# The opening of the attention stage: order of its loads, its first norm, its late tiles and the place of batch 1's norm

## The chip, the core and the metric

One core of a Trainium2 chip runs the whole kernel in one launch. TensorE (PE) multiplies matrices into PSUM, eight banks of 512 float32 columns on 128 partitions. VectorE (DVE) and ScalarE (ACT) read PSUM; GpSimd (POOL) works on SBUF and requests gathers; SyncE (SP) issues most transfers. Each engine runs its own instructions in the order in which they were written and waits on semaphores. The metric is the device time of the launch in microseconds; the median of three runs of the kernel before is 1331.42.

## The reference

Four batches of 512 tokens with 512 features go through four gated blocks. The third is cross attention, and the change lies where the second, a mixture of experts with a shared expert, passes over to it.

```
x = x + tanh(g_ffn[0]) * ffn0(layernorm(x))         # 8 routed experts, top 2, and a shared one
x = x + tanh(g_xattn[1]) * xattn(layernorm(x), ctx)  # 32 heads of 16
x = x + tanh(g_ffn[1]) * ffn1(layernorm(x))          # 8 experts, top 2

xattn: q = rope(x @ Wq, pos);  k, v = split(ctx @ Wkv);  k = rope(k)
       w = softmax(q k^T / 4) per head;  out = (w v) @ Wout + bout
```

## The kernel before

X (16 tiles of 128 tokens, four per batch) stays in SBUF. The stage before leaves three things to `attention`: the routed rows in DRAM (`f_y`), which each tile still has to gather (two rows per token) and add; the shared expert of the last eight tiles ("late tiles", numbered 0 to 7 in `LateTiles`, tiles 8 to 15 of X), whose turned input lies in DRAM (`f_xT`, two halves of 1 MB); and K and V.

`Combine` gathers and adds the routed rows. Its `pool` (L1576) makes POOL request two gathers of 256 KB per tile into one of `ring` pairs of buffers; a request waits until the tile that last used the pair is added. Its `vector` (L1590) adds them on VectorE, L1594 and L1596.

A late tile goes through `up` (PE, four products, L1961), `silu` (ACT, L1969), `gate` (VectorE, L1975), `turn` (PE, L1980), `take` (ACT, L1987), `down` (PE, two products, L1995) and `add` (VectorE, L2003). In the table `LATE` they stand as u, g, t, d and y, per turn and slot. The inputs of the late tiles are loaded into `a_attnT` and `a_wo`.

Attention works in 16 units (b, c): batch b, eight heads c. Its program is a chain of turns (b, c) from (-1, 0) to (4, 0), each with 8 steps or 16 slots. In turn (b, c) PE makes the scores of unit (b, c) (L2830), ACT their exponentials (L2986), PE the values (L2864); beside them PE makes the maximum products of the next units (L2849), two products per slot, which VectorE reduces (L3191). Maximum products of unit (0,0) begin in slot 8 of turn (-1,2), scores in turn (0,0). `jobs` puts side jobs into slots: q is the projection (L2765, q of unit (0,0) in turn (-1,1)), x the transposes of the normalized rows (L2759), m the transposes of the cut maxima (L2771), o and a those of the output, p the output projection (L2789). All but p of the last batch go through PSUM bank 7, so that each waits for the one before it to be copied out.

q of a unit is scaled by ACT (`a_qf`, L2958), its pairs are swapped (VectorE, L3093), it is rotated with the table `a_tab` and cut into three bf16 parts (`rotate_and_cut`, L1908 to L1921; VectorE for the first unit, POOL for all others), stored by SP and loaded again as `a_Q`. For the first unit ACT issues half of these loads, after which it has to load the table of Silu (L1969).

On VectorE a turn's tasks hang in slots. A turn with a norm has statistics of a tile in slots 0 to 3 (L3053), the aggregate in 4 (L3060), reciprocal and normalization in 8 (L3065, L3071), and in 12 `add_bias`: scale `a_tbias` once (L3078), which waits for its load, and add it to the batch (L3081). ACT's Sqrt is in step 3 (L3001). `batch_to_norm` gives batch 0 to turn (-1,0), batch 1 to (-1,3), batch 2 to (0,3), batch 3 to (1,3). `tiles_to_add` gives two routed tiles, in slots 10 and 14, to (-1,0), (-1,1) and to (0,0) up to (0,3).

SP's opening loads are f_xT's first half, Wq (1 MB), the rotation table (512 KB), twelve pieces of K and one of V for unit 0 (64 KB each and 512 KB), the same for unit 1, tbias and f_xT's second half.

## Time and profile before

| | us |
|---|---|
| median of 3 runs | 1331.42 |
| lowest, highest | 1329.64, 1335.47 |
| the profiled execution | 1335.91 |
| its span | 1334.1 |
| PE busy in the span | 1174.2 |
| DVE, ACT, POOL busy | 830.4, 666.2, 397.7 |

Times in the rows are microseconds from the start of the span, of one profiled execution. The stage of attention begins at 569.53 in it. A float32 product of 128x512 shows as two MATMUL records. PEclk is the granted clock of TensorE as a share of 2.4 GHz: 0.50 is the 1.2 GHz level. The chain of waits is followed back from the last instruction. A busy engine doesn't tell by itself what bounds a stretch; the rows are read for what ended each wait.

### The profile page before, as it was taken

The page shows a single profiled execution, that of the slowest core. Times are in us where ns is not written, and L with a number is a line of the kernel's source. Part 1 is how long each engine was busy: PE and PEld are TensorE (multiplying, and loading weights), DVE is VectorE, ACT ScalarE, POOL GpSimd, SP SyncE. Part 2 cuts the span into 40 slices and gives each one's busy share as a digit, 9 for nine tenths or more (in the row PEclk, how much of TensorE's full clock was granted, in tenths as well). Part 3 has the DMA queues.
Part 4 walks back from the last instruction along what each step waited for, and adds up shares of the span by engine and source line. Part 5 has one row for each costly group of instructions (what it writes and reads, how often), then busy time and mean ns, then how long its engine had stood idle before and what let it go on. Part 6 is the DMA issues. An engine that isn't in the chain of part 4 may idle for free.

```text
span 1334.1 us, 16599 instructions
## 1 busy us (share of the span) xinstructions
PE 1174.2 (88%) x5308; PEld 511.9 (38%) x5309; DVE 830.4 (62%) x1283; ACT 666.2 (50%) x1175; POOL 397.7 (30%) x469
## 2 busy tenths in 40 slices
PE   5776876897999999958799989999999999889998
PEld 3454443564444444423232223222322222234543
DVE  6787865244455554135988888778777777624543
ACT  2575564564222222235456666566656556662453
POOL 4455631001222222033234432222223233101332
PEclk8988997999899999977999999999999999998999
DMA  7324125654444444194324342222222225300011
GB/s 247 129 91 134 56 95 195 223 192 159 150 147 154 147 147 135 56 277 112 113 85 132 116 124 72 85 81 81 68 85 80 81 81 66 46 0 9 33 40 48
DMA packets 111029, 145.79 MB, mean 109 GB/s; under 512 B 24952, under 2 KB 79736, under 8 KB 110440
## 3 DMA queue, kind: packets, MB, share of 16 engines
q1 hardware_dynamic: 91816, 113.47, 26.6%
q0 software_dynamic: 18368, 28.85, 8.4%
q10 hardware_dynamic: 768, 2.49, 0.5%
q8 instruction: 42, 0.69, 0.2%
q14 instruction: 35, 0.29, 0.1%
HBM read 99.54 MB, written 48.37 MB: 111 GB/s over the span
## 4 chain that ended last, share of the span: by engine, by line
PE 33%; DVE 8%; issue 8%; ACT 7%; POOL 1%; DMA 0%; ACTq 0%; POOLq 0%; DVEq 0%
PE PS L2864 8%; PE PS L2830 6%; PE PS L2765 5%; PE PS L2849 4%; PE PS L2789 3%; DVE a_top L3191 3%; ACT shared_w L2986 3%; PE PS L2368 2%; ACT a_E L2986 2%; PE PS L2391 1%; PE PS L1961 1%; POOL a_K L2128 1%; DVE a_early L3071 1%; PE PS L2759 1%; DVE X L3139 0%
## 5 line engine op out<-in xcount | busy, mean ns | idle before, releaser
L3191 DVE TENSOR_REDUCE a_top<-PS 128x2 f32<-128x1024 f32 x256 | 308.8, 1223 | 89.5 <-PE PS L2849 83.2
L2830 PE MATMUL PS<-a_Q,a_K 99*128 99x512 bf16 (+1 forms) x512 | 167.5, 387 | 18.7 <-ACT a_E L2986 4.2
L2986 ACT ACTIVATE shared_w<-PS 128x512 f32<-128x512 f32 x256 | 138.8, 596 | 80.1 <-PE PS L2830 77.2
L2986 ACT ACTIVATE a_E<-PS 128x512 f32<-128x512 f32 x256 | 138.9, 596 | 63.0 <-PE PS L2830 59.7
L1481 PE MATMUL PS<-f_W,f_GT 128*128 x312 | 141.8, 598 | 0.0
L2849 PE MATMUL PS<-a_K,a_Q 64*128 64x512 bf16 x512 | 100.4, 389 | 7.8 <-DVE a_top L3191 7.2
L2830 PEld LDWEIGHTS PS<-a_Q,a_K 99*128 99x128 bf16 (+1 forms) x512 | 44.5, 98 | 155.2 <-issue 50.8
L1908 POOL TENSOR_TENSOR a_qf<-a_qf,a_tab 128x512 f32<-128x512 f32 x15 | 19.1, 1272 | 282.3 <-DVE a_swapped L3093 282.3
L1537 DVE TENSOR_TENSOR f_H<-f_SG,PS 128x256 f32<-128x256 f32 x39 | 16.4, 421 | 125.5 <-ACT f_SG L1521 125.5
L1481 PEld LDWEIGHTS PS<-f_W,f_GT 128*128 128x128 f32 x312 | 57.0, 193 | 57.3 <-issue 57.3
L2765 PE MATMUL PS<-a_xT,a_early 128*128 128x512 f32 x128 | 72.3, 661 | 2.1 <-ACT a_xT L2952 0.7
L1500 PE MATMUL PS<-f_W,f_HT 128*128 x156 | 73.2, 593 | 0.0
L2789 PE MATMUL PS<-a_wo,a_attnT 128*128 128x512 f32 x128 | 70.5, 657 | 1.4 <-ACT a_attnT L2974 0.8
L1521 ACT ACTIVATE f_SG<-PS 128x256 f32<-128x256 f32 x39 | 15.0, 384 | 110.2 <-PE PS L1481 110.2
L2864 PE MATMUL PS<-shared_w,a_V 128*32 128x512 f32 x512 | 69.7, 617 | 0.0
L2864 PE MATMUL PS<-a_E,a_V 128*32 128x512 f32 x512 | 68.7, 609 | 0.0
L2849 PEld LDWEIGHTS PS<-a_K,a_Q 64*128 64x128 bf16 x512 | 24.6, 93 | 111.2 <-issue 69.7
L2128 POOL TENSOR_TENSOR a_K<-a_Q,a_tab 128x512 bf16<-128x512 f32 x32 | 33.3, 1041 | 108.7 <-DVE a_Q L2228 108.7
L2368 PE MATMUL PS<-a_early,a_Q 128*128 128x512 bf16 x256 | 60.5, 379 | 0.0
L1527 ACT COPY f_Y<-PS 128x512 f32<-128x512 f32 x39 | 22.9, 587 | 60.4 <-PE PS L1500 60.4
L2228 DVE TENSOR_TENSOR a_Q<-a_Q,PS 128x512 f32<-128x512 f32 x32 | 22.0, 686 | 47.2 <-ACT a_Q L2289 47.2
L1447 POOL DMA_INDIRECT f_G<-f_xn,f_idx x39 | 41.9, 1073 | 29.5 <-POOL f_idx L1444 28.7
(379 smaller groups left out, 2058.1 us busy)
## 6 DMA issues: line engine op xcount, KB each, us to landing
f0r_raw<-in_L_ffn_W_dram SPq DMA_DIRECT2D x24, 512.0 KB, 4.5
a_K<-k_parts SPq DMA_DIRECT2D x192, 64.0 KB, 2.3
a_Q<-a_q_parts SPq DMA_DIRECT2D x186, 64.0 KB
f_y<-f_Y SPq DMA_DIRECT2D x39, 256.0 KB
v_units<-V SPq DMA_DIRECT2D x16, 512.0 KB, 2.9
a_V<-v_units SPq DMA_DIRECT2D x16, 512.0 KB, 3.6
k_parts<-f_k_parts SPq DMA_DIRECT2D x16, 384.0 KB, 3.4
a_q_parts<-a_parts SPq DMA_DIRECT2D x16, 384.0 KB, 2.8
```

What stands on the lines that cost most here:

```text
L1447: pool.indirect_dma_start(out=G[k][:], out_offset=None, in_=xn_dram, in_offset=bass.IndirectOffsetOnAxis(ap=idx[:, k:k + 1].bitcast(U32), ...
L1481: last = nc.tensor.matmul(PS[:, 2 + k % 2, 0:2 * I], GT[k][:, c, :], W13[:, bass.ds(e, 1), c, :].rearrange("p a n -> p (a n)"), start=(c = ...
L1500: last = nc.tensor.matmul(PS[:, 6 + k % 2, :], HT[k][:, c, :], W2[:, bass.ds(e, 1), c, :].rearrange("p a n -> p (a n)"), start=(c == 0), s ...
L2128: self.nc.gpsimd.tensor_tensor(self.H[j % 2][:, h * HE:(h + 1) * HE, :], self.HF[h], gate, ALU.mult).then_inc(self.h_ready, 1)
L2368: last = nc.tensor.matmul(PS[:, 2 * h + m, :], self.xb[b % 2][:, c, t * P:(t + 1) * P], self.W13[:, c, m, h * HE:(h + 1) * HE, :].rearrang ...
L2765: last = nc.tensor.matmul(B, wq[:, extra, c * P:(c + 1) * P], xT[:, extra, :], start=(extra == 0), stop=(extra == DC - 1))
L2789: last = nc.tensor.matmul(bank_of(kind, unit, extra), attnT[b % 2][:, d, t * P:(t + 1) * P], wo[:, d, :], start=(d == 0), stop=(d == DC - 1))
L2830: nc.tensor.matmul(PS[:, 4 + h % 2, :], K6[k][0:rows_, o, head // 2, kt * P:(kt + 1) * P], Q6[k][0:rows_, o, head // 2, :], start=True, st ...
L2849: last = nc.tensor.matmul(PS[:, 2 * pair + o, :], Q6[k][at, o, h // 2, t * P:(t + 1) * P], K6[k][at, o, h // 2, :], start=True, stop=True)
L2864: last = nc.tensor.matmul(PS[32 * h:32 * h + 32, 6, :], V[k][:, kt, (step // 4) * 4 + h, :], E[step % 2][:, h, :], start=(kt == 0), stop=( ...
L2986: nc.scalar.activation(E[step % 2][:, h, :], PS[:, 4 + h % 2, :], ACT.Exp).then_inc(exp_done, 1)
L3191: nc.vector.tensor_reduce(top[:, h - h % 2:h - h % 2 + 2, t], PS[:, 2 * pair:2 * pair + 2, :], AX.X, ALU.max).then_inc(maxed, 1)
```

## The change

- `Combine` in attention gets four pairs of buffers instead of three.
- SP waits for the first tile's add before it issues Wq, and for the third tile's before the rotation table and all that follows. The second half of f_xT moves ahead of unit 1's K and V; tbias stays behind them and is now last.
- Each half of f_xT is loaded in four pieces with a semaphore each, and `up` waits per piece.
- VectorE takes the statistics of batch 0 behind each tile's adds, and aggregates and normalizes before its first turn. Gate 0 stands behind tile 1, gate 1 behind tile 2.
- The x transposes of batch 0 alternate between banks 7 and 3. Late tile 2's down product goes to bank 6 instead of 2; the first maximum products wait for three late adds.
- In `LATE` only half of tile 2's `up` is done before the turns; it and the other tiles stand later.
- Batch 1's norm moves from turn (-1,3) to (0,0), its x transposes to slots 10, 12, 13, 14. The routed adds of (0,0) to (0,3) move to (0,1) to (1,0).

```diff
-    DOWN = (6, 0, 1, 2, 6, 6, 6, 6)
+    DOWN = (6, 0, 1, 6, 6, 6, 6, 6)
...
     def load(self, sp, k):
-        sp.dma_start(self.homes[k], self.xT_dram[k]).then_inc(self.loaded[k], 16)
+        for c in range(self.DC):
+            sp.dma_start(self.homes[k][:, c, :], self.xT_dram[k][:, c, :]).then_inc(self.loaded[k][c], 16)
...
-        if c == 0:
-            if t == 0:
-                pe.wait_ge(self.loaded[k], 16)
-            if n >= 2:
-                pe.wait_ge(self.HT_ready, n - 1)
+        if t == 0:
+            pe.wait_ge(self.loaded[k][c], 16)
+        if c == 0 and n >= 2:
+            pe.wait_ge(self.HT_ready, n - 1)
...
-        rows = Combine(nc, sb, sem, X, F32, weights, pos, ffn_gate, ys, 3, [attnT[1][:, d, :] for d in range(DC)])
+        rows = Combine(nc, sb, sem, X, F32, weights, pos, ffn_gate, ys, 4, [attnT[1][:, d, :] for d in range(DC)])
...
-                for d, when in enumerate((6, 7, 8, 10)):
+                for d, when in enumerate((10, 12, 13, 14) if b == 0 else (6, 7, 8, 10)):
...
-        LATE = {(-1, 0): {9: [("g", 2, 0), ("y", 0, 0), ("y", 1, 0), ("t", 2, 0)]},
...
+        LATE = {(-1, 0): {9: [("y", 0, 0), ("y", 1, 0)]},
+                (-1, 2): {4: ups(2, [2, 3]) + ups(3), 5: [("g", 2, 0), ("t", 2, 0)] + downs(2), 7: [("y", 2, 0), ("g", 3, 0)],
...
+            if kind == "x" and unit[0] == 0:
+                return PS[:, (7, 3)[extra % 2], :]
...
-            nb = {0: b + 1 if b == -1 else None, DC - 1: b + 2}.get(c)
+            nb = {0: b + 1 if b < 1 else None, DC - 1: b + 2 if b >= 0 else None}.get(c)
...
-            if b == -1 and c < 2 or b == 0:
-                first = TB + 2 * c if b == -1 else 2 * TB + 2 * c
+            turn_ = DC * b + c
+            if -DC <= turn_ < 2 - DC or 0 < turn_ <= DC:
+                first = TB + 2 * c if b == -1 else 2 * TB + 2 * (turn_ - 1)
...
             late.load(sp, 0)
+            sp.wait_ge(rows.tile_added, 1)
             sp.dma_start(wq, Wq.rearrange("(c p) n -> p c n", p=P)).then_inc(wq_loaded, 16)
...
+                    else:
+                        sp.wait_ge(rows.tile_added, TB - 1)
                     sp.dma_start(tab[0][:], tables_dram[bass.ds(unit[0], 1)].rearrange("a p k s -> p (a k) s")).then_inc(tab_loaded, 16)
...
                     load_kv(unit)
+                    late.load(sp, 1)
                     load_kv((0, 1))
...
                     sp.dma_start(tbias[:], bout.partition_broadcast(P)).then_inc(tbias_loaded, 16)
-                    late.load(sp, 1)
...
+                    if b == 0 and extra >= 2:
+                        pe.wait_ge(xT_ready, extra - 1)
...
-                        pe.wait_ge(late.added, 3 + pair)
+                        pe.wait_ge(late.added, 3)
...
+            def first_tile(t):
+                rows.vector(v, t)
+                v.wait_ge(rows.tile_added, t + 1)
+                first_norm.step(nc.vector.bn_stats(stats[:, t, :], X[:, t, :]))
...
-            rows.vector(v, 0)
+            first_tile(0)
+            first_tile(1)
             late.gate(v, 0)
-            rows.vector(v, 1)
+            first_tile(2)
             late.gate(v, 1)
-            rows.vector(v, 2)
-            rows.vector(v, 3)
+            first_tile(3)
+            first_norm.wait()
+            for t in range(TB):
+                last = nc.vector.bn_aggr(mv[:, t, :], stats[:, t, :])
...
-                        at(t, stat)
+                        if nb:
+                            at(t, stat)
...
-                    at(4, aggregate)
-                    at(8, normalize)
+                    if nb:
+                        at(4, aggregate)
+                        at(8, normalize)
                     at(12, add_bias)
```

The order of the instructions, first SP at the opening of attention (`a_attnT` and `a_wo` are the homes of f_xT's halves, `a_early` of Wq), before:

```order
L1949 DMA a_attnT<-f_xT 128x2048
L2643 DMA a_early<-in_L_xattn_Wq_dram 128x4x512
L2667 DMA a_tab<-rope_tables 128x1024
L2655 DMA a_K_0<-k_parts 16x4x512 x12
L2656 DMA a_V<-v_units 128x1024
L2655 DMA a_K_1<-k_parts 16x4x512 x12
L2656 DMA a_V<-v_units 128x1024
L2676 DMA a_tbias<-in_L_xattn_bout_dram 128x512
L1949 DMA a_wo<-f_xT 128x2048
L2683 DMA a_q_parts<-a_parts 128x3x512
```

and now:

```order
L1950 DMA a_attnT<-f_xT 128x512 x4
L2650 DMA a_early<-in_L_xattn_Wq_dram 128x4x512
L2676 DMA a_tab<-rope_tables 128x1024
L2662 DMA a_K_0<-k_parts 16x4x512 x12
L2663 DMA a_V<-v_units 128x1024
L1950 DMA a_wo<-f_xT 128x512 x4
L2662 DMA a_K_1<-k_parts 16x4x512 x12
L2663 DMA a_V<-v_units 128x1024
L2686 DMA a_tbias<-in_L_xattn_bout_dram 128x512
L2692 DMA a_q_parts<-a_parts 128x3x512
```

The second half of f_xT moved ahead of K_1; tbias is the last load ahead of the store of q's parts.

VectorE from the normalization of batch 0 (`a_early` is written) to the first rotation, before:

```order
L3071 TENSOR_SCALAR a_early<-X,a_mv,a_rstd 128x512 x4
L1975 TENSOR_TENSOR a_E<-a_E,PS 128x256
L2003 SCALAR_TENSOR_TENSOR X<-PS,tg,X 128x512 x2
L1594 SCALAR_TENSOR_TENSOR X<-a_attnT,a_tw,X 128x512
L1596 SCALAR_TENSOR_TENSOR X<-a_attnT,a_tw,X 128x512
L3078 TENSOR_SCALAR a_tbias<-a_tbias,tg 128x512
L3081 TENSOR_TENSOR X<-X,a_tbias 128x2048
L1594 SCALAR_TENSOR_TENSOR X<-a_rows,a_tw,X 128x512
L1596 SCALAR_TENSOR_TENSOR X<-a_rows,a_tw,X 128x512
L3093 STREAM_SHUFFLE a_swapped<-a_qf 128x512
L1908 TENSOR_TENSOR a_qf<-a_qf,a_tab 128x512
```

and now:

```order
L3053 TENSOR_SCALAR a_early<-X,a_mv,a_rstd 128x512 x4
L2003 SCALAR_TENSOR_TENSOR X<-PS,tg,X 128x512 x2
L1594 SCALAR_TENSOR_TENSOR X<-a_attnT,a_tw,X 128x512
L1596 SCALAR_TENSOR_TENSOR X<-a_attnT,a_tw,X 128x512
L3106 TENSOR_SCALAR a_tbias<-a_tbias,tg 128x512
L3109 TENSOR_TENSOR X<-X,a_tbias 128x2048
L1594 SCALAR_TENSOR_TENSOR X<-a_attnT,a_tw,X 128x512
L1596 SCALAR_TENSOR_TENSOR X<-a_attnT,a_tw,X 128x512
L3122 STREAM_SHUFFLE a_swapped<-a_qf 128x512
L1908 TENSOR_TENSOR a_qf<-a_qf,a_tab 128x512
L1909 TENSOR_TENSOR a_swapped<-a_swapped,a_tab 128x512
```

The bias (tbias, then X<-X,a_tbias) and one more tile's adds stand ahead of the shuffle in both.

TensorE around the first maximum products (`a_K_0,a_Q_0`), before:

```order
L1961 MATMUL PS<-shared_w,a_attnT 128x512 x4
L1961 MATMUL PS<-shared_w,a_wo 128x512 x4
L1980 MATMUL PS<-identf,a_E 128x128 x2
L1995 MATMUL PS<-shared_w,a_E 128x512 x2
L1980 MATMUL PS<-identf,a_E 128x128 x2
L2849 MATMUL PS<-a_K_0,a_Q_0 128x512 x2
L1995 MATMUL PS<-shared_w,a_E 128x512
L2849 MATMUL PS<-a_K_0,a_Q_0 128x512 x2
L1995 MATMUL PS<-shared_w,a_E 128x512
L2849 MATMUL PS<-a_K_0,a_Q_0 128x512 x2
L1961 MATMUL PS<-shared_w,a_wo 128x512
```

and now:

```order
L2770 MATMUL PS<-identf,a_early 128x128 x16
L2776 MATMUL PS<-a_xT,a_early 128x512 x8
L1961 MATMUL PS<-shared_w,a_attnT 128x512 x6
L1980 MATMUL PS<-identf,a_E 128x128 x2
L1995 MATMUL PS<-shared_w,a_E 128x512 x2
L2860 MATMUL PS<-a_K_0,a_Q_0 128x512 x2
L1980 MATMUL PS<-identf,a_E 128x128 x2
L1961 MATMUL PS<-shared_w,a_wo 128x512
L2860 MATMUL PS<-a_K_0,a_Q_0 128x512 x2
L1995 MATMUL PS<-shared_w,a_E 128x512 x2
L2860 MATMUL PS<-a_K_0,a_Q_0 128x512 x2
L1961 MATMUL PS<-shared_w,a_wo 128x512
```

Late tile 3's and 4's up products (`shared_w,a_wo` is 4's) left the place ahead of the maximum products; tile 2's turn and down products came there.

## Rows read from the trace of the kernel before

**Rows 1.** The page's part 4: the chain that ended last, shares of the span by engine.

```profile
PE 33%; DVE 8%; issue 8%; ACT 7%; POOL 1%; DMA 0%; ACTq 0%; POOLq 0%; DVEq 0%
```

**Rows 2.** A stretch: busy of PE, PEld, DVE, ACT, POOL; PE clock, DMA share, GB/s.

```profile
600.00:610.00 10.00, 6.67 (x20) 4.13 (x21) 8.20 (x12) 4.48 (x6) 2.97 (x2) 0.50 0.54 197
```

**Rows 3.** Order of time: start, length (us), engine, line, form, count, idle before.

```profile
580.67 0.75 DVE L1594 SCALAR_TENSOR_TENSOR X<-a_attnT,a_tw,X 128x512 f32<-128x512 f32 x1 [10.87 <-DMA a_attnT<-f_y,l_pos]
...
594.05 0.75 DVE L1594 SCALAR_TENSOR_TENSOR X<-a_attnT,a_tw,X 128x512 f32<-128x512 f32 x1 [4.85 <-DMA a_attnT<-f_y,l_pos]
...
601.00 1.11 PE L2759 MATMUL PS<-identf,a_early 128*128 128x128 f32 x4 [7.88 <-DVE a_early L3071]
```

**Rows 4.** Order of time, the first rotation on VectorE, its first and last step.

```profile
615.59 0.01 DVE L3093 LOAD_MASK_SELECT a_swapped<-a_qf  x1 [7.25 <-ACT a_qf L2958]
...
620.22 0.69 DVE L1921 TENSOR_TENSOR a_parts<-a_qf,a_parts 128x512 bf16<-128x512 f32 x1
```

**Rows 5.** Groups by line, VectorE, 631.5 to 676.8: count, busy us, mean ns, idle.

```profile
L3191 DVE TENSOR_REDUCE a_top<-PS 128x2 f32<-128x1024 f32 x24 | 28.9, 1217 | 3.2 <-issue 1.9 <-PE PS L2849 1.3
L3053 DVE BATCH_NORM_STATS2 a_stats<-X 128x6 f32<-128x512 f32 x4 | 2.7, 684 | 0.0
L3071 DVE TENSOR_SCALAR a_early<-X,a_mv,a_rstd 128x512 f32<-128x512 f32 x4 | 2.3, 629 | 0.0
```

**Rows 6.** Order of time, TensorE, from the first maximum products to the first score.

```profile
631.55 0.39 PE L2849 MATMUL PS<-a_K,a_Q 64*128 64x512 bf16 x2
...
634.84 1.13 PE L1961 MATMUL PS<-shared_w,a_wo 128*128 128x512 f32 x2
...
676.87 0.59 PE L2830 MATMUL PS<-a_Q,a_K 99*128 99x512 bf16 x2 [0.55 <-ACT a_E L1987]
```

**Rows 7.** Order of time, POOL's request; and a page row, landing time last.

```profile
583.74 0.95 POOL L1582 DMA_INDIRECT a_attnT<-f_y,l_pos  x1 [0.30 <-issue]
...
f_G<-f_xn,f_idx POOLq DMA_INDIRECT x39, 4.1
```

**Rows 8.** SP's issues in order; VectorE at tbias; landing times (us, last number).

```profile
577.99 8.12 SPq L2655 DMA_DIRECT2D a_K<-k_parts  x12
...
586.72 2.77 SPq L2676 DMA_DIRECT2D a_tbias<-in_L_xattn_bout_dram  x1
...
603.96 0.48 DVE L3078 TENSOR_SCALAR a_tbias<-a_tbias,tg 128x512 f32<-128x512 f32 x1
...
a_K<-k_parts SPq DMA_DIRECT2D x192, 64.0 KB, 2.3
...
a_early<-in_L_xattn_Wq_dram SPq DMA_DIRECT2D x1, 1024.0 KB, 10.9
a_tbias<-in_L_xattn_bout_dram SPq DMA_DIRECT2D x1, 256.0 KB, 16.9
```

**Rows 9.** One of eleven stretches of 2 us from 581 to 603, columns as in rows 2.

```profile
583.00:585.00 2.00, 1.52 (x6) 0.52 (x4) 0.56 (x1) 0.65 (x2) 1.38 (x2) 1.00 1.13 187
```

**Rows 10.** Order of time, ScalarE, behind the first rotation.

```profile
626.33 1.28 ACT L1969 ACT_TABLE_LOAD   x1 [0.87 <-issue]
```

**Rows 11.** Turns (0,0), (0,2), (0,3), (1,2), (1,3) as stretches.

```profile
677.70:708.70 31.00, 29.97 (x158) 9.67 (x156) 25.38 (x30) 21.24 (x41) 12.84 (x14) 1.00 0.18 49
...
738.90:769.50 30.60, 28.49 (x154) 8.11 (x152) 26.27 (x32) 19.86 (x38) 12.28 (x14) 1.00 0.38 112
769.50:805.40 35.90, 30.43 (x154) 8.23 (x152) 31.46 (x45) 22.61 (x41) 10.77 (x12) 0.95 0.38 104
...
872.70:905.10 32.40, 31.75 (x160) 9.48 (x160) 24.10 (x29) 19.86 (x39) 8.99 (x10) 1.00 0.26 79
905.10:940.90 35.80, 33.47 (x160) 9.55 (x160) 30.81 (x43) 22.60 (x42) 9.04 (x10) 0.95 0.22 72
```

**Rows 12.** Order of time, ScalarE, the load behind the Sqrt of turn (0,3).

```profile
782.41 1.28 ACT L2986 ACT_TABLE_LOAD   x1
```

35 lines of the change are left out of this document (22 added, 13 removed).

## The prediction

> **What bounds the kernel now.** The page's list of the chain comes first [rows 1]: of the chain that ended last TensorE has 33% of the span and no other engine over 8%. The kernel goes from hand to hand between engines, so an edit is worth what it takes off one stretch of that chain. The change touches 569.53 to about 709 us and, lightly, the turns up to 840.
>
> Next the stretches of 10 us: in attention's opening PE is at 6.67 of 10 us and at half clock, 0.50 [rows 2], and the 2 us stretches before it have the DMA engines full [rows 9]. The order of time shows why [rows 3]. The first routed rows are added at 580.67, after 10.87 us of waiting for a DMA, and tile 3's at 594.05; its two gathers were requested only at 582.48 and 583.74, since a ring of three buffers made them wait. From there a serial chain: statistics, Sqrt, norm, x transposes from 601.00, q and its copy qf, for which VectorE waited until 615.59, the rotation, ended at 620.22 + 0.69 = 620.91 (I call this T) [rows 4], q stored and loaded, the first maximum product (L2849) at 631.55, the first score (L2830) at 676.87 [rows 6].
>
> Last the stretch from 631.55 to 676.87, 45.3 us. VectorE has 24 reductions of 1.22 us (29.3), batch 1's norm (four statistics 2.7, normalization 2.3, in the same view bias 2.3, aggregate and reciprocal 0.5: 7.8), the cut of the maxima 3.1, a shuffle 0.7, three gates and two late adds 2.8: 43.7 of 45.3. VectorE bounds it [rows 5].
>
> **The change part by part.**
>
> Gathers. Each request holds POOL 0.95 us with 0.30 between [rows 7]. The second request of tile t now starts at 571.48 + 2.51t, t = 0 to 3. Landing is bounded by two rows: 4.1 us, the median of the same gather in the stage before, and 10.3 us, tile 3's from 583.74 to 594.05 under the loads [rows 3, 7]. I take 4.1, since only the 1 MB of f_xT is now beside the first ones: 575.6, 578.1, 580.6, 583.1. By the Trainium skill (DMA: Bandwidth & Descriptors, Anatomy of one DMA) a 256 KB transfer on this path would be about 2.0 + 0.6 = 2.6 us, an estimate from its fit; the trace's 4.1 is used, and the page's figure would bring the rows 1.5 us earlier and the sum to -3.5.
>
> First norm. A tile costs VectorE two adds of 0.75 and one statistic of 0.62. Tile 3 is added at 584.7; then 0.7 + 0.4 + Sqrt 0.3 + 0.2 + 1.9 us give the normalized rows at 589 to 590, against 601.0: 11 us. Four transposes in two banks hide three copies of 0.59, some 1.9 us. PE has been idle for 7.88 us before 601.00 and runs at the 1.2 GHz level (0.50); now it works until about 589, so 2.4 GHz is likely. qf could be ready at 597.6 at full clock, 602.5 at half, against 615.5 [rows 4]. If the chain went on from there, T would fall by 13 to 18 us.
>
> The held-back loads. It does not go on. VectorE's order of issue has the bias addition of batch 0 (L3078, L3081) and tile 5's adds ahead of the rotation, both before and now, and the bias waits for the tbias load, now SP's last. Before, tbias landed at 586.72 + 16.9 = 603.6 and was taken at 603.96, no wait to speak of; VectorE then stood idle 7.25 us until qf [rows 4, 8]. Now SP waits for tile 2's add (580.6 + 1.5 = 582.2), and then issues tab, twelve K_0, V, four pieces of f_xT, twelve K_1, V, tbias. Queued behind that wait is everything SP does; who waits for it is VectorE, through tbias.
> When does tbias land? Lower bound, by issue: 0.5 + 6.3 + 0.5 + 2.1 + 6.3 + 0.5 + 0.5 = 16.7 us and 2.3 to land: 601 [rows 8]. By the engines: from Wq's landing (569.90 + 10.9 = 580.8) to tbias at 603.6 they were full, 22.8 us: in all eleven stretches of 2 us the share is 0.96 to 1.17, in the one shown 1.13 at only 187 GB/s, which is the K loads [rows 8, 9]. In that time they carried tab, both K and V sets, tbias and about 14 gathers. Now the same, plus 1 MB of f_xT and minus about 4 gathers (1 MB): equal. 582.2 + 22.8 = 605.0; a tail of Wq, now requested at 577, adds 0.5: 605.5. Upper bound: the gathers save nothing and the 1 MB of f_xT goes at 187 GB/s, 5.6 us: 610.6. I take 605.5, because the engines were full in every stretch of it.
> Then VectorE needs 4.4 us (scale, bias, tile 5: 603.96 to 608.34) and 5.3 us (rotation: 615.59 to 620.91) [rows 4, 8]. T = 615.2: **5.7 us gained, not 13 to 18**. What is late next is tbias; tab, Wq, rows and K_0 are hidden under it.
>
> From T to the first score. Before it took 55.96 us. Up to ACT's table load (5.4 us after T) nothing changes [rows 10]. Then PE must do tile 2's turn and two down products, as it did tile 3's, but it has been idle since about 607 and I price them at half clock: 3.4 instead of 1.98, and tile 2's add (0.74) now stands ahead of the first maximum product. It comes 12.9 us after T, 10.6 before. The stretch behind it loses the 7.8 us of norm on VectorE, which leaves it 37.8. But late tiles moved in: PE now has 24 pairs of maximum products at 0.32, 28 products at 1.06 (16 up, 8 down, 4 q; before 22), five turns at 0.45 and the turn of the maxima at 0.38: 40.0 us, and PE is the bound. With three waits of 0.3 for gates, 1.5 for the last two slots, which VectorE sets, and 1 of half clock: 43.4 [rows 5, 6]. Sum 56.3, against 55.96: **0.3 lost**. The first score is at 671.5, 5.4 us earlier.
>
> Norm of batch 1 in turn (0,0). Turns by their stretches [rows 11]: (0,0) 31.0, (0,2) 30.6, (0,3) 35.9 with a norm and two routed adds, (1,2) 32.4, (1,3) 35.8 with a norm alone. A norm costs 3.4 without adds and 5.3 with them. The adds leave (0,0), so I take 3.4, bounds 0 (VectorE has 5.6 us idle in it) and 5.3. The two tiles move to (1,0), whose turn has no norm: 0, hidden by VectorE's idle time as in (0,0), at most 1.9 = 5.3 - 3.4. The Sqrt comes into the exponentials: in (0,3) a table load at 780.80, Sqrt, another load at 782.41 to 783.69, 2.9 us in all [rows 12]; this is inside the 3.4.
> The Trainium skill (ScalarE: Activation LUTs, Table sets: the hidden batching unit) speaks against this move: calls should be batched by set. It prices exp, then sqrt, at 5.3 us for two loads. The row shows 2.9; by the page's price the turn would cost 2.4 more and the sum be +0.4. No run here shows the extra.
>
> Edits with one answer: tile 2's product in bank 6, four sets of row buffers, one SP issue made four, ACT's silu of tile 2 after the turns: nothing; all lie under the waits named.
>
> **Sum.** -5.4 + 3.4 = -2.0 us. The profiled execution took 1335.91 (span 1334.1), 4.5 over the median of the runs; 1333.9 for it, and from the median 1331.42 - 2.0 = 1329.4.
>
> **The rivals.**
> A, gain kept: tbias lands at 601 to 602, because gathers end early and SP's issue sets the pace. T gains 10, the clock has stayed high (2 us more), the norm costs 2: -9 to -10 us, 1322. For: the lower bound above. Against: full engines in [rows 9].
> B, the change doesn't reach its aim: eight requests outstanding land no faster than before (10.3 us each). Tile 2's add is then at 588, tbias at 611, T at 620.7: 0.2 gained there, 0.3 lost up to the score and 3.4 in the turn: +3.5 us, 1335.
> C, slower: VectorE held in front of the rotation by tbias for longer than it used to wait for qf, and the norm at its full price. tbias after 611.2 puts T beyond 620.91, and each us later is lost. At 613.5 T is 623.2; with the turn at 5.3 and (1,0) at 1.9: 2.3 + 0.3 + 5.3 + 1.9 = +9.8, 1341. It becomes slower than before from tbias at 607.5, with the turn at 3.4.
>
> **How the numbers follow.** Forecast (-6 to +2) 0.53; A 0.23; B 0.14; C 0.10. A measurement of this kernel tells about 0.5%, 6.7 us, from no change. A is mostly beyond it, and a fringe of the forecast with it: faster 0.27. C and part of B: slower 0.12. Same 0.61. The range takes A's end and B's: 1319 to 1338.
>
> **What would show each step.** Row adds on VectorE at about 576, 578, 581, 584; x transposes near 590, 0.6 us each. Then VectorE idle before L3106 until about 605, released by tbias's DMA; the rotation right behind tile 5's adds, no wait for qf. T near 615, first L2860 near 628, first L2841 near 671.5. Between them VectorE with gaps and PE near full. Turn (0,0) near 34.4, with two table loads. The forecast is wrong if L3106 starts before 602, or if the turns grow by more than 5.3.

## The result

The changed kernel took 1338.16 us (median of 4 runs, 1335.03 to 1342.39) beside 1330.57 for the kernel before on the same chip: ratio 1.0048, 95% interval 1.0028 to 1.0068. Run again on another occasion (below) it took 1332.98 and the ratio came to 1.0016, 0.9994 to 1.0039. So it is slower by 0.5% on the first occasion and by nothing clear of noise on the second, where -0.15% was forecast. The first time lies just outside the range of 1319 to 1338, the second inside it.

The profiled execution of the changed kernel took 1335.03 (span 1333.3), the shortest of the four. Its stage of attention begins at 567.95, where SyncE issues the first piece of f_xT, against 569.53 before. Whatever is compared below is counted from that instant.

VectorE in order of time (start, length, engine, line, operation, operands, count; in brackets the idle time before it and what ended it):

```profile
575.10 0.75 DVE L1594 SCALAR_TENSOR_TENSOR X<-a_attnT,a_tw,X 128x512 f32<-128x512 f32 x1 [6.87 <-DMA a_attnT<-f_y,l_pos]
...
584.90 0.75 DVE L1594 SCALAR_TENSOR_TENSOR X<-a_rows,a_tw,X 128x512 f32<-128x512 f32 x1 [2.55 <-DMA a_rows<-f_y,l_pos]
...
606.97 0.49 DVE L3106 TENSOR_SCALAR a_tbias<-a_tbias,tg 128x512 f32<-128x512 f32 x1 [14.08 <-DMA a_tbias<-in_L_xattn_bout_dram]
607.49 2.29 DVE L3109 TENSOR_TENSOR X<-X,a_tbias 128x2048 f32<-128x2048 f32 x1
...
611.28 0.72 DVE L3122 STREAM_SHUFFLE a_swapped<-a_qf 128x512 f32<-128x512 f32 x1
...
615.88 0.69 DVE L1921 TENSOR_TENSOR a_parts<-a_qf,a_parts 128x512 bf16<-128x512 f32 x1
```

The rows do what the change meant: tile 3 is added from 17.0 us behind the stage's start instead of 24.5 [rows 3]. Then VectorE stands for 14.08 us in front of L3106, and what ends the wait is tbias's DMA. The rotation has no wait of its own; it begins behind tile 5's adds and ends at 616.57, 48.6 behind the start, against 51.4 in [rows 4].

SyncE's issues show why tbias is late:

```profile
576.66 0.39 SPq L2650 DMA_DIRECT2D a_early<-in_L_xattn_Wq_dram  x1
581.33 0.32 SPq L2676 DMA_DIRECT2D a_tab<-rope_tables  x1
581.69 6.24 SPq L2662 DMA_DIRECT2D a_K<-k_parts  x12
...
597.04 0.46 SPq L2686 DMA_DIRECT2D a_tbias<-in_L_xattn_bout_dram  x1
```

TensorE in the same stretch, up to turn (0,0):

```profile
593.45 3.67 PE L2776 MATMUL PS<-a_xT,a_early 128*128 128x512 f32 x8 [0.72 <-ACT a_xT L2962]
...
604.74 5.31 PE L1961 MATMUL PS<-shared_w,a_attnT 128*128 128x512 f32 x12
624.20 0.69 PE L1980 MATMUL PS<-identf,a_E 128*128 128x128 f32 x2 [14.14 <-DVE a_E L1975]
625.35 3.78 PE L1995 MATMUL PS<-shared_w,a_E 128*128 128x512 f32 x4 [0.46 <-ACT a_E L1987]
630.07 0.61 PE L2860 MATMUL PS<-a_K,a_Q 64*128 64x512 bf16 x2 [0.94 <-DVE X L2003]
...
673.89 3.23 PE L2776 MATMUL PS<-a_xT,a_early 128*128 128x512 f32 x4
676.91 2.37 PE L1995 MATMUL PS<-shared_w,a_E 128*128 128x512 f32 x4
```

q was done early and at full clock, and TensorE then idled 14.14 us. The first maximum product stands 13.5 us behind the rotation's end, the first score (673.04) 56.5 behind it. Turns (0,0) and (0,1) from q to q (duration, busy time of PE, PEld, DVE, ACT, POOL, then granted clock, DMA share, GB/s):

```profile
673.89:710.48 36.59, 32.72 (x157) 10.28 (x157) 29.69 (x40) 24.24 (x44) 13.91 (x14) 0.91 0.30 93
710.48:741.93 31.45, 29.24 (x151) 8.06 (x152) 25.03 (x31) 19.85 (x38) 13.40 (x14) 0.95 0.34 102
```

Turn (0,0) took 31.0 at clock 1.00 before [rows 11]. The change thus gives back 5.6 us in one turn, 1.2 in the next, after it won 2.25 up to the first score. The page's list of the chain now has the load in it:

```profile
PE 32%; DVE 9%; issue 7%; ACT 6%; DMA 1%; SPq 1%; POOL 1%; ACTq 0%; POOLq 0%; DVEq 0%
PE PS L2875 7%; PE PS L2841 5%; PE PS L2776 4%; PE PS L2860 4%; DVE a_top L3220 3%; PE PS L2800 3%; PE PS L2368 2%; ACT shared_w L2996 2%; ACT a_E L2996 2%; PE PS L2391 1%; PE PS L1995 1%; SPq L2662 1%; DMA a_tbias<-in_L_xattn_bout_dram 1%; PE PS L1961 1%; POOL a_K L2128 1%
```

### The profile page after: what moved, and what is told of

The parts are those of the page before. It is cut to its first block, busy times and chain, and to the rows that moved or that the text cites. A ratio compares the mean times of both kernels' runs of the same rounds, so it can differ in the third digit from the quotient of the medians.

```text
span 1333.3 us, 16543 instructions
## 1 busy us (share of the span) xinstructions
PE 1164.8 (87%) x5247; PEld 509.0 (38%) x5309; DVE 829.2 (62%) x1283; ACT 666.2 (50%) x1175; POOL 399.4 (30%) x469
## 4 chain that ended last, share of the span: by engine, by line
PE 32%; DVE 9%; issue 7%; ACT 6%; DMA 1%; SPq 1%; POOL 1%; ACTq 0%; POOLq 0%; DVEq 0%
PE PS L2875 7%; PE PS L2841 5%; PE PS L2776 4%; PE PS L2860 4%; DVE a_top L3220 3%; PE PS L2800 3%; PE PS L2368 2%; ACT shared_w L2996 2%; ACT a_E L2996 2%; PE PS L2391 1%; PE PS L1995 1%; SPq L2662 1%; DMA a_tbias<-in_L_xattn_bout_dram 1%; PE PS L1961 1%; POOL a_K L2128 1%
## 5 line engine op out<-in xcount | busy, mean ns | idle before, releaser
L2841 PE MATMUL PS<-a_Q,a_K 99*128 99x512 bf16 (+1 forms) x468 | 158.1, 390 | 19.3 <-ACT a_E L2996 6.2
L2800 PE MATMUL PS<-a_wo,a_attnT 128*128 128x512 f32 x128 | 67.8, 635 | 1.5 <-ACT a_attnT L2984 0.8
L1527 ACT COPY f_Y<-PS 128x512 f32<-128x512 f32 x39 | 22.8, 586 | 60.5 <-PE PS L1500 60.5
L2228 DVE TENSOR_TENSOR a_Q<-a_Q,PS 128x512 f32<-128x512 f32 x32 | 21.9, 685 | 47.2 <-ACT a_Q L2289 47.2
```

Source lines behind the costliest of these rows:

```text
L2800: last = nc.tensor.matmul(bank_of(kind, unit, extra), attnT[b % 2][:, d, t * P:(t + 1) * P], wo[:, d, :], start=(d == 0), stop=(d == DC - 1))
L2841: nc.tensor.matmul(PS[:, 4 + h % 2, :], K6[k][0:rows_, o, head // 2, kt * P:(kt + 1) * P], Q6[k][0:rows_, o, head // 2, :], start=True, st ...
```

## The experiments

Kernels whose name begins with a_ are the changed kernel with an edit, those with b_ the kernel before with an edit. The numbers are us behind the stage's start in each one's profiled execution: the start of tile 3's adds, VectorE's use of tbias, the rotation's end, the first score, and the q products of turn (1,1), behind which all turns have the same work. The expectations call this last one the q products of unit (1,1). These times are called anchors below. The ratio is the time over that of the kernel before, run beside it, with its 95% interval.

| | tile 3 | tbias | rotation | score | turn (1,1) | ratio |
|---|---|---|---|---|---|---|
| before, profiled | 24.5 | 34.4 | 51.4 | 107.3 | 270.8 | |
| before_again | 21.6 | 32.9 | 48.4 | 104.3 | 267.6 | 0.9997 (0.9975 to 1.0019) |
| after, profiled | 17.0 | 39.0 | 48.6 | 105.1 | 274.6 | 1.0048 (1.0028 to 1.0068) |
| after_again | 17.2 | 38.9 | 48.5 | 105.1 | 274.5 | 1.0016 (0.9994 to 1.0039) |
| a_tbias_first | 17.7 | 25.6 | 38.9 | 94.3 | 263.8 | 0.9935 (0.9913 to 0.9958) |
| a_bias_later | 17.1 | 41.5 | 38.6 | 93.6 | 260.8 | 0.9935 (0.9910 to 0.9959) |
| b_tbias_first | 21.3 | 31.2 | 48.3 | 104.3 | 267.4 | 1.0001 (0.9979 to 1.0022) |
| b_loads_held | 17.3 | 40.6 | 50.2 | 107.8 | 270.9 | 1.0030 (1.0015 to 1.0046) |
| b_four_buffers | 19.9 | 35.2 | 46.9 | 104.0 | 266.8 | 0.9980 (0.9962 to 0.9999) |
| a_loads_early | 18.5 | 41.4 | 38.6 | 95.0 | 263.5 | 0.9946 (0.9920 to 0.9972) |
| a_three_buffers | 17.2 | 41.1 | 38.3 | 93.2 | 260.5 | 0.9939 (0.9918 to 0.9959) |
| b_norm_moved | 21.4 | 32.6 | 48.2 | 99.9 | 267.3 | 1.0005 (0.9991 to 1.0018) |
| a_norm_back | 16.8 | 37.6 | 47.2 | 106.2 | 271.0 | 1.0074 (1.0049 to 1.0099) |
| a_both | 17.0 | 24.9 | 38.8 | 96.8 | 261.1 | 0.9938 (0.9919 to 0.9957) |
| a_no_root | 16.9 | 40.1 | 37.1 | 93.4 | 263.4 | not compared |
| a_tile2_early | 16.8 | 24.7 | 36.9 | 90.7 | 260.1 | 0.9913 (0.9895 to 0.9931) |
| a_tile2_norm_back | 16.8 | 24.7 | 36.9 | 96.0 | 260.6 | 0.9907 (0.9876 to 0.9937) |

### Does tbias hold the rotation?

Theory: it does, since its consumer stands ahead of the rotation on VectorE. Rivals: the full DMA engines hold the chain and tbias is only where it shows; or the order of the other loads matters. First the load is moved, in the changed kernel:

```diff
                     else:
                         sp.wait_ge(rows.tile_added, TB - 1)
+                        sp.dma_start(tbias[:], bout.partition_broadcast(P)).then_inc(tbias_loaded, 16)
                     sp.dma_start(tab[0][:], ...)
...
-                if is_first(unit):
-                    sp.dma_start(tbias[:], bout.partition_broadcast(P)).then_inc(tbias_loaded, 16)
```

> The changed kernel with one line moved: tbias is loaded ahead of tab instead of behind both K sets. Times are counted from the stage's start (SyncE's first f_xT load); in the changed kernel the rotation ends 48.6 us behind it, the first score stands at 105.1 and the q products of unit (1,0) at 142.5. Theory, the wait for tbias holds the chain: VectorE no longer waits for tbias, rotates as soon as qf is there (31.7), and the rotation ends at 37 to 40. Behind it the way to the first score (56.5) stays, less what the loads of K_1 still hold back: first score 5 to 9 us earlier, turn (0,0) unchanged at 36.6, time 5 to 9 us less than the changed kernel. Rival 1, the DMA engines hold the chain and tbias is only where it shows: q's store and its twelve loads land behind K_1, so the first maximum product comes at most 3 us earlier. Rival 2, tbias itself needs 10 us or more to land wherever it is requested: VectorE waits until 592 or later, but qf at 599 hides that, and the result is as in the theory.

VectorE of a_tbias_first:

```profile
593.56 0.48 DVE L3105 TENSOR_SCALAR a_tbias<-a_tbias,tg 128x512 f32<-128x512 f32 x1
...
601.51 0.01 DVE L3121 LOAD_MASK_SELECT a_swapped<-a_qf  x1 [3.57 <-ACT a_qf L2967]
```

The wait is gone, and now the rotation waits for qf. It ends 9.8 us earlier (38.85 against 48.62), the first score comes 10.8 earlier, a little more than expected; 1322.75 us against 1332.37 for the kernel before. The first maximum product comes 9.3 us earlier (52.9 against 62.1), so rival 1 (at most 3 us) is out. The second edit leaves every load where it was and moves the consumer:

```diff
-                    at(12, add_bias)
+                    if nb:
+                        at(12, add_bias)
+                    else:
+                        later.append(add_bias)
...
+                if (b, c) == (-1, 1):
+                    at(15, later[0])
```

> The changed kernel, its loads untouched (tbias last, behind both K sets), but batch 0's bias addition put behind the rotation and the adds of tiles 6 and 7 on VectorE. Theory, the wait for tbias holds the rotation: the rotation ends at 37 to 40 us behind the stage's start, as with tbias loaded first (38.9), VectorE stands waiting for tbias behind it, where it holds only the shuffle of unit (0,1), and the time is that of the run with tbias first, 0.9935 of the kernel before, give or take 0.2%. Rival, tbias first gained because K_0, K_1 or q's loads came otherwise: the time stays near the changed kernel's, 1.005.

In order of time on VectorE of a_bias_later, the bias addition has become a matter between other work:

```profile
602.21 0.01 DVE L3129 LOAD_MASK_SELECT a_swapped<-a_qf  x1 [6.72 <-ACT a_qf L2968]
...
610.35 0.48 DVE L3107 TENSOR_SCALAR a_tbias<-a_tbias,tg 128x512 f32<-128x512 f32 x1
```

The rotation ends at 38.6 and the ratio is that of a_tbias_first to the fourth digit, with tbias as late as ever: requested at 598.3, it took 10.1 us to land, 39.5 behind the stage's start. (It was said that VectorE would wait for tbias behind the rotation; it did not, tbias had landed.) So the place of the consumer in VectorE's order made the wait, and neither the DMA engines nor the order of K_0, K_1 and q's loads. The same load moved in the kernel before is the control:

```diff
+                    if is_first(unit):
+                        sp.dma_start(tbias[:], bout.partition_broadcast(P)).then_inc(tbias_loaded, 16)
                     sp.dma_start(tab[0][:], ...)
...
-                    sp.dma_start(tbias[:], bout.partition_broadcast(P)).then_inc(tbias_loaded, 16)
```

> The kernel before with the tbias load ahead of tab and nothing else, the counterpart of the same edit in the changed kernel. Theory, the wait counts only where tbias comes after qf: in the kernel before VectorE took tbias at 34.4 and then still stood 7.25 us until qf, so the bias addition goes into idle time either way: the rotation ends at 51.4 +- 3 (the gathers' landing varies by 3 us between executions) and the time is within 0.2% of before. Rival, tbias loaded first makes the whole opening quicker (its 128 descriptors no longer stand behind the K loads'): rotation at 46 or less, time 4 us less or more.

```profile
599.51 0.48 DVE L3079 TENSOR_SCALAR a_tbias<-a_tbias,tg 128x512 f32<-128x512 f32 x1
...
611.25 0.01 DVE L3094 LOAD_MASK_SELECT a_swapped<-a_qf  x1 [7.35 <-ACT a_qf L2959]
```

Nothing, 1.0001: VectorE stands 7.35 us for qf behind it here, and 7.25 in the kernel before.

### How much of the rotation's gain was there at all?

The two controls b_tbias_first and b_norm_moved ended the rotation at 48.3 and 48.2, though nothing ahead of it differs from the kernel before in a way that counts; its profiled execution had 51.4. Both kernels were therefore run again.

> The changed kernel, unaltered, for a second profile and more times on the chip of the next three. Its profiled execution had the shortest of its times (1335.0), the others go up to 1342.4; in the run with the norm back the profiled one is 8 us shorter than four others. Theory, the landing of tbias varies from execution to execution, and with it everything, as long as VectorE waits for it: the rotation ends anywhere between 48 and 57 us behind the stage's start, and the time varies by 8 us, where the run with tbias first varies by 6. Rival, the spread is that of TensorE's clock: the rotation ends at 48.6 +- 1 again and the time differs where nothing was changed.

> The kernel before, unaltered, run as if it were a change. Theory, the profiled execution of before was a late one: the gathers of tiles 0 and 3 land up to 3 us earlier in another, the rotation ends at 48 to 50 behind the stage's start instead of 51.4, and the q products of unit (1,1) stand at 266 to 269 instead of 270.8. Rival, 51.4 is the kernel's value, and the 48.2 and 48.3 of two other runs are due to their edits: it comes at 51 to 52 again. The ratio should be 1 within 0.2%.

VectorE of before_again:

```profile
590.66 0.75 DVE L1594 SCALAR_TENSOR_TENSOR X<-a_attnT,a_tw,X 128x512 f32<-128x512 f32 x1 [2.19 <-DMA a_attnT<-f_y,l_pos]
...
612.14 0.01 DVE L3093 LOAD_MASK_SELECT a_swapped<-a_qf  x1 [5.76 <-ACT a_qf L2958]
```

The first expectation's theory fell: the opening of the changed kernel comes out the same to 0.1 us (48.6, 48.5), though the two executions took 1335.03 and 1340.62. a_norm_back, whose opening is the same, has tbias at 37.6 and the rotation's end at 47.2: tbias's landing moves by 1.4 us in three executions, not by 8. The second held. The execution on which the forecast was built was late: three others of the kernel before's opening end the rotation at 48.2 to 48.4 and have turn (1,1) at 267.3 to 267.6. Against these the changed kernel wins nothing up to the rotation, and stands 6.9 us later at turn (1,1). This is near the first ratio (+6.4 us) and above the second (+2.1).

The rest of the spread lies in work that no edit touches. From the q products of turn (3,0) to the span's end it is 258.1 us in the changed kernel's first profile, 262.5 in its second, 261.1 in before's, 262.7 in before_again's, 258.0 in a_bias_later's. The stretch from 1200 to 1240 of the changed kernel, first and second profile:

```profile
1200.00:1240.00 40.00, 36.35 (x168) 17.69 (x164) 18.05 (x36) 12.38 (x19) 8.54 (x10) 1.00 0.02 8
```

```profile
1200.00:1240.00 40.00, 36.42 (x148) 16.88 (x150) 16.73 (x34) 11.90 (x19) 7.50 (x9) 0.91 0.02 8
```

The granted clock is 1.00 in one and 0.91 in the other, 0.91 in the kernel before's and 0.94 in before_again. Of the eleven profiles of the changed kernel and its variants nine have 256.4 to 259.4 us here and two 262.5; of the six of the kernel before and its variants one has 258.1 and five 261.1 to 263.7. Whether an edit has a part in that, or chance, is not settled; the 4.4 us are more than what the ratios of a_bias_later and a_tile2_early show beyond their anchors against before_again (1.9 and 4.1 us). A difference of 0.3% is therefore read from the anchors here.

### Which part of the change makes q early?

```diff
             late.load(sp, 0)
+            sp.wait_ge(rows.tile_added, 1)
...
+                    else:
+                        sp.wait_ge(rows.tile_added, TB - 1)
...
                     load_kv(unit)
+                    late.load(sp, 1)
                     load_kv((0, 1))
...
-                    late.load(sp, 1)
```

> The kernel before with only the loads held back (Wq behind the first add, tab and K_0 behind the third, f_xT's second half between the K sets, tbias last). Theory: rows come earlier (tile 3 added near 20 us behind the stage's start instead of 24.5), but tbias lands at 38 to 40 instead of under 34.4, the bias addition waits for it, and the rotation ends at 47 to 50, as in the changed kernel, against 51.4: the whole change up to the rotation is in this part. Time 0 to 4 us less than before. Rival, the four buffers are needed: tile 3 is added after 24 and tbias lands after 42, the rotation ends at 51 to 54, time +0 to +3.

```profile
608.94 0.49 DVE L3081 TENSOR_SCALAR a_tbias<-a_tbias,tg 128x512 f32<-128x512 f32 x1 [9.44 <-DMA a_tbias<-in_L_xattn_bout_dram]
```

In the kernel before, holding the loads back alone moves tile 3 from 21.6 to 17.3 and tbias from 32.9 to 40.6, and the rotation waits for it: 50.2 against before_again's 48.4. The times forecast for each point were about right; that it would be a gain was read off the late 51.4. It costs 0.3%, where 0 to 4 us of gain were expected. The fourth buffer alone:

```diff
-..., weights, pos, ffn_gate, ys, 3, [attnT[1][:, d, :] for d in range(DC)])
+..., weights, pos, ffn_gate, ys, 4, [attnT[1][:, d, :] for d in range(DC)])
```

> The kernel before with four row buffers instead of three and nothing else. Theory: tile 3's two requests start 5 us earlier but land under the loads (10 us each before), so tile 3 is added 1 to 5 us earlier, the rotation with it, tbias (landed by 34.4) holds nothing: the rotation ends at 47 to 50 against 51.4, time 1 to 4 us less. Rival, more requests beside the K loads only divide the same bandwidth: tile 3 is added at 24.5 as before and nothing changes, +-1 us.

It moves tile 3 to 19.9 and the rotation to 46.9, and gains 0.2%, with an interval that ends just under 1. (The 21.3 that the next expectation names for it was the start of its statistics, not of tile 3's adds.) From the other side, in a_bias_later, the loads are put back to their order of before, or the fourth buffer is taken away:

```diff
             late.load(sp, 0)
-            sp.wait_ge(rows.tile_added, 1)
...
-                    else:
-                        sp.wait_ge(rows.tile_added, TB - 1)
...
-                    late.load(sp, 1)
                     load_kv((0, 1))
...
                     sp.dma_start(tbias[:], ...).then_inc(tbias_loaded, 16)
+                    late.load(sp, 1)
```

> The changed kernel with the bias addition behind the rotation and SyncE's loads in the order of before (nothing held back; tbias behind both K sets, ahead of f_xT's second half). It tells what the holding back is worth once tbias holds nothing. Theory, the held-back loads make the rows land early: without them tile 3 is added at 21.3 (as with four buffers alone) instead of 16.9, the normalized rows follow 4 to 5 us later, and the rotation ends at 43 to 46 instead of 38.6; time 0.997 to 0.999 of before. Rival, four requests at once and statistics per tile do all of it: the rotation ends at 40 or less and the time is 0.9935.

```diff
-..., weights, pos, ffn_gate, ys, 4, [attnT[1][:, d, :] for d in range(DC)])
+..., weights, pos, ffn_gate, ys, 3, [attnT[1][:, d, :] for d in range(DC)])
```

> The changed kernel with the bias addition behind the rotation, and three row buffers instead of four. Theory, the fourth buffer matters little once the loads are held back: tile 3's two requests wait for tile 0's add (7.2 behind the start) and start by 10 to 12 instead of 6 to 9, tile 3 is added at 17 to 20 instead of 16.9, and the rotation ends at 38.6 to 41; the statistics per tile, the two banks and late tile 2's smaller share ahead of q make the rest; time 0.9935 to 0.995. Rival, the fourth buffer is what makes the rows early: tile 3 is added after 21, the rotation ends after 42, time 0.997.

Neither alone matters for the rotation: 38.6 and 38.3 against 38.6. With the loads early the rows are 1.4 us later and the rotation is not, so the expectation's rival came. The first score is then 1.5 us later (95.0 against 93.6) and turn (1,1) 2.7, and the ratio of 0.9946 doesn't tell this from 0.9935. No run takes both away. The rest is on the engines. From the start of the x transposes to q TensorE needs:

```profile
592.64 1.10 PE L2767 MATMUL PS<-identf,a_early 128*128 128x128 f32 x8 [1.15 <-DVE a_early L3050]
594.07 1.12 PE L2767 MATMUL PS<-identf,a_early 128*128 128x128 f32 x8 [0.33 <-ACT a_xT L2959]
595.91 3.67 PE L2773 MATMUL PS<-a_xT,a_early 128*128 128x512 f32 x8 [0.72 <-ACT a_xT L2959]
```

in a_loads_early, and in before_again

```profile
597.61 1.12 PE L2759 MATMUL PS<-identf,a_early 128*128 128x128 f32 x4 [4.73 <-DVE a_early L3071]
...
602.99 1.12 PE L2759 MATMUL PS<-identf,a_early 128*128 128x128 f32 x4 [0.25 <-ACT a_xT L2952]
604.83 6.57 PE L2765 MATMUL PS<-a_xT,a_early 128*128 128x512 f32 x8 [0.72 <-ACT a_xT L2952]
```

q begins 27.0 behind the start in the one and 35.75 in the other. Of these 8.7 us, 3.0 are the rows (tile 3's adds start at 18.5 against 21.6), 1.7 the statistics (from tile 3's adds' start to the transposes' 5.2 against 6.95), and 3.9 the transposes: 3.3 us to q with two banks at full clock, 7.2 with one bank at half clock and tile 2's turn between (granted clock 1.00 and 0.50). No run takes the banks, the clock and the turn apart. A further 2.9 are q itself at full clock, 3.67 instead of 6.57; but in a_bias_later, with q at half clock (6.09), the rotation ends at 38.6 as well: in a_loads_early ScalarE's three fills of K and Q rows stand ahead of qf and end at 601.45, 1.9 us after q.

### What does batch 1's norm cost in turn (0,0)?

Pairs of kernels differ by its place alone (with the two tiles' adds and the x slots that go with it):

```diff
-            nb = {0: b + 1 if b < 1 else None, DC - 1: b + 2 if b >= 0 else None}.get(c)
+            nb = {0: b + 1 if b == -1 else None, DC - 1: b + 2}.get(c)
...
-            turn_ = DC * b + c
-            if -DC <= turn_ < 2 - DC or 0 < turn_ <= DC:
-                first = TB + 2 * c if b == -1 else 2 * TB + 2 * (turn_ - 1)
+            if b == -1 and c < 2 or b == 0:
+                first = TB + 2 * c if b == -1 else 2 * TB + 2 * c
...
-                for d, when in enumerate((10, 12, 13, 14) if b == 0 else (6, 7, 8, 10)):
+                for d, when in enumerate((6, 7, 8, 10)):
```

> The changed kernel with batch 1's norm back in the turn before unit (0,0)'s, the two tiles' adds back in (0,0) and the x transposes in their old slots. Theory, the norm costs more in turn (0,0) than it saves ahead of the first score: turn (0,0) from q to q falls from 36.6 to 31.0 and (0,1) from 31.45 to 30.2, 6.8 us together; ahead of the first score VectorE gets 7.8 us of work back, which PE's late products hide in part: 2 to 4 us later. Net 3 to 5 us less than the changed kernel. Rival 1, the turn is long because TensorE runs at half clock in it, which the norm has no part in: turn (0,0) stays over 34 and the sum is slower than the changed kernel by 0 to 3 us. Rival 2, the 7.8 us come back in full: net -1 to +1.

> The changed kernel with both edits: tbias loaded ahead of tab, batch 1's norm back in the turn before. If the two causes are separate and both real, the gains add: 8 to 14 us less than the changed kernel, 2 to 7 us less than the kernel before. If the window ahead of the first score is set by VectorE, an earlier rotation still moves its start, and they add all the same. If the DMA engines hold the first maximum product (rival 1 of the tbias run), it equals the run with the norm back, give or take 1 us.

> The kernel before with only batch 1's norm moved into turn (0,0), the tiles' adds one turn later and the x transposes in slots 10, 12, 13, 14. Theory, the norm costs 5 to 7 us in turns (0,0) and (0,1) (31.0 to 36 or 37, 30.2 to 31.5), and ahead of the first score VectorE, which bounds that stretch in the kernel before (43.7 of 45.3 us), is relieved of 7.8 us, of which 4 to 7 show: between -2 and +3 us in all. Rival, the turn's growth in the changed kernel comes from tile 7 and the clock: turn (0,0) grows by at most 3.4 and the kernel gets 2 to 4 us faster.

Between the first score and turn (1,1) lie 163.3 us in before_again and 167.4 in b_norm_moved: the norm costs 4.1 there. Between the rotation's end and the first score lie 55.9 and 51.7: it saves 4.2. Net nothing, and 1.0005. In the changed order, where late products fill that stretch, it costs 4.6 (a_norm_back, 164.8 against 169.5) and 5.2 (a_both, 164.3 against 169.5 in a_tbias_first), and saves 2.5 (59.0 against 56.5 and 58.0 against 55.5). Turn (0,0) of a_norm_back takes 32.2, not the expected 31.0. In a_both the gains add, as expected: 261.1 against 274.6. By the anchors the norm ahead of the first score is thus 2 to 3 us better; the times don't show it (0.9938 beside 0.9935, and 1.0074 beside 1.0048, where even the sign is the other). a_norm_back's own anchors say 3.5 us less than the changed kernel, its time 3 us more; its profiled execution took 1332.99, the other four 1340.34 to 1342.44. What these four had that the profiled one did not is not known.

Turn (0,0) of b_norm_moved:

```profile
668.69:703.60 34.91, 31.10 (x157) 9.72 (x157) 29.54 (x40) 24.35 (x44) 14.99 (x14) 0.95 0.26 78
```

34.9 against 31.0, where later turns with a norm take 35.8 and 35.9 [rows 11]. The clock of 0.95 is part of these 3.9 us: in b_norm_moved it is 0.67 from 682.8 to 687.8. The 1.7 us more of the changed kernel lie at the turn's start, at a clock of 0.66 from 673 to 678: its first four q records took 3.23 instead of 1.98 and the down products 2.37 instead of 1.88. In after_again these take 1.98 and 1.88 again, the turn has clock 0.95, and still takes 35.95; turn (0,1) takes 30.2 instead of 31.45, so the 1.2 us there belong to the one execution.

What in the norm costs? The root is left out:

```diff
+                        if nb == 1:
+                            nc.scalar.copy(sd[:], mv[:, :, 1]).then_inc(sd_ready, 1)
+                        else:
-                        nc.scalar.activation(sd[:], mv[:, :, 1], ACT.Sqrt, bias=ln_eps[:]).then_inc(sd_ready, 1)
+                            nc.scalar.activation(sd[:], mv[:, :, 1], ACT.Sqrt, bias=ln_eps[:]).then_inc(sd_ready, 1)
```

> The changed kernel with the bias addition behind the rotation, and batch 1's root left out (a copy in place of the Sqrt, so the normalization of batch 1 is not the reference's); its statistics and its normalization stay. It prices the two table loads in turn (0,0), which lasts 35.2 from q to q with the root and 31.0 without any norm. Theory, most of the norm's price is the interruption of the exponentials by load, Sqrt, load (2.9 us): turn (0,0) falls to 31.5 to 32.5. Rival, it is VectorE's 7.8 us of norm work: the turn stays at 34 or more. By the Trainium skill's price for the pair of table loads (5.3 us) the turn would fall below 30.

The turn took 36.67, no less than the 35.15 with the root in a_bias_later. There load, Sqrt and load stood from 674.93 to 677.84, and VectorE waited 2.16 us for TensorE behind them; without them VectorE has no gap from 668.55 to 687.4. The normalization that the x transposes wait for begins 2.0 us earlier behind the turn's start (19.8 against 21.8), but it now falls beside POOL's rotation of the next unit and ends only 0.8 earlier. VectorE and POOL of a_no_root, the first two of four operations:

```profile
682.08 0.88 DVE L3103 TENSOR_SCALAR a_early<-X,a_mv,a_rstd 128x512 f32<-128x512 f32 x1
682.88 1.36 DVE L3103 TENSOR_SCALAR a_early<-X,a_mv,a_rstd 128x512 f32<-128x512 f32 x1
```

```profile
682.06 0.62 POOL L1919 TENSOR_SCALAR a_parts<-a_qf 128x512 bf16<-128x512 f32 x1 [0.16 <-POOL a_qf L1916]
682.76 1.20 POOL L1921 TENSOR_TENSOR a_parts<-a_qf,a_parts 128x512 bf16<-128x512 f32 x1
```

and VectorE of a_bias_later, all four:

```profile
685.07 1.92 DVE L3100 TENSOR_SCALAR a_early<-X,a_mv,a_rstd 128x512 f32<-128x512 f32 x4
```

The four took 3.08 us instead of 1.92, TensorE idled 2.9 in front of the transposes, and its clock then fell to half:

```profile
685.00:690.00 5.00, 4.69 (x18) 1.72 (x19) 3.65 (x4) 1.57 (x3) 2.17 (x3) 0.50 0.48 143
```

So the theory (31.5 to 32.5) fell and the rival (34 or more) came, in one execution. The root is not what keeps the turn long: its 2.9 us gave 2.0 at the normalization's start, and 1.2 of them were lost beside POOL, more at the half clock behind it. That VectorE's share of the norm is what lengthens the turn fits its lack of gaps, but no run shows it by itself, and what the loads cost where they bound the path stays open. The Trainium skill (ScalarE: Activation LUTs, Table sets: the hidden batching unit) prices a pair at some 5.3 us; the pair here lasted 2.9 with its Sqrt, and the turn did not fall below 30.

### What is late next, and a kernel that beats both

With tbias out of the way the first maximum product stood 14 us behind the rotation, and was thought to be held by late tile 2. Besides the tbias load ahead of the table, as in a_tbias_first, this kernel has:

```diff
-        LATE = {(-1, 0): {9: [("y", 0, 0), ("y", 1, 0)]},
-                (-1, 2): {4: ups(2, [2, 3]) + ups(3), 5: [("g", 2, 0), ("t", 2, 0)] + downs(2), 7: [("y", 2, 0), ("g", 3, 0)],
+        LATE = {(-1, 0): {9: [("y", 0, 0), ("y", 1, 0)], 11: [("s", 2, 0)], 15: [("g", 2, 0)]},
+                (-1, 1): {4: [("t", 2, 0)]},
+                (-1, 2): {4: downs(2) + ups(3), 5: [("y", 2, 0)], 7: [("g", 3, 0)],
...
-            for c in range(2):
+            for c in range(DC):
                 late.up(pe, 2, c)
...
-            FILLS = {(-1, 0): {11: [(1, 0)], 12: [(1, 1)], 13: [(1, 2)]}, (-1, 1): {4: [(1, 3)]},
+            FILLS = {(-1, 0): {11: [(1, 0)], 12: [(1, 1)]}, (-1, 1): {4: [(1, 2), (1, 3)]},
...
-                        if kind == "u" and part == DC - 1:
+                        if kind == "s" or kind == "u" and part == DC - 1:
```

> The changed kernel with tbias loaded ahead of tab, and late tile 2 taken out of the way of the first maximum product: its up product wholly ahead of the x transposes, silu and gate in the turn before, its transposition behind q, its down products ahead of tile 3's up products. With tbias first the rotation ends at 38.9, and the first maximum product stands at 52.9, 14 us behind it, though q's parts should have landed by 47 or 48: it waits for tile 2's add, and that for table load, silu, gate, transposition and two down products at half clock. Theory, tile 2 is what is late next: the first maximum product comes at 47 to 49 and the first score 3 to 5 us earlier than 94.3, time 2 to 5 us less than with tbias first (0.990 to 0.992 of before). Rival, the stretch behind it is bound by TensorE, which has the same products to do: the first maximum product comes earlier but the first score by under 1.5 us, time within 1 us of the tbias run.

TensorE of a_tile2_early:

```profile
605.38 3.60 PE L1961 MATMUL PS<-shared_w,a_attnT 128*128 128x512 f32 x8
615.78 0.61 PE L2860 MATMUL PS<-a_K,a_Q 64*128 64x512 bf16 x2 [6.81 <-DMA a_Q<-a_q_parts]
```

The first maximum product comes at 47.1 and the first score 3.7 us earlier than in a_tbias_first, as the theory had it, but not by tile 2 alone. The edit also puts one of ScalarE's three fills behind qf, and q ran at full clock (3.7 us, where it took 5.9 in a_tbias_first), so the rotation ends 2.0 us earlier (36.9 against 38.9); from there the first maximum product takes 10.3 us instead of 14.0, and the first score 53.8 instead of 55.4. So 1.7 us are left for tile 2, near the rival's 1.5: TensorE has the same products to do there. The ratio is 0.9913, 1321.7 us against 1332.58; its interval overlaps that of a_tbias_first. What is late now is q's own way through memory: TensorE stands 6.81 us for it. The norm put back ahead of it:

> The changed kernel with tbias first, late tile 2 out of the way, and batch 1's norm back in the turn ahead of unit (0,0)'s. Three pairs so far: the norm in turn (0,0) costs 4 to 5 us in turns (0,0) and (0,1), and saves 3.0 to 4.3 ahead of the first score; the times don't tell them apart. Theory, a net of 0 to 2.7 us for the norm ahead: the q products of unit (1,1) stand at 257.5 to 260 against 260.1, time 0.989 to 0.9915. Rival, with tile 2 out of the way VectorE bounds the stretch ahead of the first score and the norm costs all of its 7.8 us there: over 261, time 0.992 or more.

260.6 against 260.1 and 0.9907 against 0.9913: no difference, and 260.6 lies between what the theory (up to 260) and the rival (over 261) named. Here the stretch from the rotation to the first score gives back all of the turn's gain (59.2 against 53.8, beside 164.6 against 169.5 behind the score). Both are faster than the kernel before by 0.9%.

## Why the prediction was wrong

- **The rows**: the forecast's times count from a stage that starts at 569.53. Behind the start its adds stand at 6.5, 8.5, 11.5 and 14.5; measured are 7.1, 9.3, 11.8 and 17.0. Nearly right for the first three, 2.5 us early for tile 3. From its second request to its add tile 0 took 5.2 us; tiles 1 and 2 were not waited for, at most 4.9; tile 3 took 7.1 (577.76 to 584.90), with Wq, requested at 576.66, beside it. So 4.1 was too short, and 10.3 far too long.
- **The first norm, transposes, q**: q at full clock, as said. The transposes began 22.2 behind the start, forecast 20.5. qf was ready at 31.7 instead of 28.1: 1.7 us of the 3.6 came from above, and 1.9 since ScalarE's fills of K and Q rows stood ahead of its copy, until 598.99 where q had ended at 597.12. Both misses hid under the wait for tbias.
- **VectorE waits for tbias in front of the rotation**: right, and shown from both sides (a_tbias_first, a_bias_later). That the 13 to 18 us of the straight chain don't arrive was right too; without the wait the rotation ended 12.5 to 12.8 us ahead of the profiled 51.4, and 9.5 to 9.8 ahead of the usual 48.4.
- **When tbias lands**: the step that failed. Forecast 605.5, which is 36.0 behind the stage's start, bounds 31.5 and 41.1; measured 39.0 and 38.9. SyncE's wait ended 0.7 us later than priced, and from there to tbias it took 25.6 us, not 22.8 and 0.5 for Wq's tail. The forecast had the engines full over the same amount ("Now the same, plus 1 MB of f_xT and minus about 4 gathers (1 MB): equal"). That they were full was right, "equal" was not. From Wq's landing to tbias before, and from SyncE's wait to tbias now:

```profile
580.80:603.60 22.80, 13.26 (x37) 6.11 (x35) 14.02 (x28) 3.95 (x8) 7.58 (x8) 0.86 1.06 284
581.33:606.97 25.64, 18.85 (x52) 8.61 (x52) 8.46 (x18) 12.19 (x12) 5.81 (x7) 0.93 1.00 282
```

  At the same rate, 284 and 282 GB/s, they moved 6.5 MB before and 7.2 MB now, and the 0.75 MB more are 2.7 us. The sum also put nothing for the order: tbias, with its 256 KB, stood at the end of everything, 9.9 us from its issue to its use. Before, f_xT's half was requested behind tbias and landed at 605.9, after it.
- **The base of 51.4**: the second step that failed. Not a term was wrong, but the execution was late: three others give 48.2 to 48.4. Against 48.4 the forecast's own 45.7 is a gain of 2.7 us instead of 5.7, and with tbias at 39.0 it was nothing. That the profiled execution took 4.5 us more than the median was on record; the terms took its rotation as the kernel's own.
- **From the rotation to the first score**: forecast 56.3, first maximum product at 12.9, the stretch behind it bound by TensorE at 43.4. Measured 56.5, 13.5 and 43.0. Right.
- **Norm in turn (0,0)**: forecast 3.4 with bounds 0 and 5.3, measured 3.9 in b_norm_moved and 5.0 to 5.6 in the two profiles of the changed kernel, and 1.2 or nothing in turn (0,1). That a norm lengthens the turn was right; its size was taken from turns at clock 0.95, and the turn of 36.6 had 0.91. In turn (1,0) the adds cost nothing, as said: 34.9 both.
- **Sum**: -5.4 + 3.4 was forecast. Against the profiled execution of before it was -2.25 + 6.0 = +3.75 at turn (1,1), against before_again +6.9. Of the 5.75 us between -2.0 and +3.75, 3.15 were missed up to the first score, nearly all of them tbias, and 2.6 behind it.
- **The rivals**: none came. B's +3.5 is near the measured +3.75, by other terms: it had tile 2 added at 588 and tbias at 611. C named the mechanism, but began to lose at tbias after 38.0 with a base of 51.4; with the usual base that point is at about 35, and the measured 39.0 is beyond it. A's 1322 is what the kernel takes once the tbias load or its consumer is moved: A failed by this one wait.
- **Profiled run over the median**: 4.5 us were taken as a constant to subtract. Some 3 of them were the opening's lateness: at turn (1,1) this execution stood 3.2 us behind before_again.

## What to carry to other kernels

When loads are held back to let an urgent one through, go through their consumers: an engine takes its work in order, so the load that is requested last holds everything that stands behind its consumer, here a rotation that has no use for a bias. Move either the load to the front or the consumer back; each gave 0.65% here, where the whole change without it gave none. And take the base of a stage from more than one profiled execution before pricing a few us in it: the opening of this kernel moves by 3 us from one to another with nothing changed.

## What the runs showed of the hardware

Several VectorE operations on SBUF waited until a POOL operation that had begun before them had ended. Of the four normalizations of a_no_root the first two took 0.88 and 1.36 us instead of 0.55, and each ended 0.28 us behind the end of the POOL operation beside it. The subtractions of 128x32 in the cut of the maxima show it more plainly, in the same kernel:

```profile
L3152 DVE TENSOR_TENSOR a_ntop<-a_ntop,a_mcut x16: 191/526/1141, 647.0 to 1140.5; 128x32 f32<-128x32 f32 x16
```

With the one behind it (L3156) it ran 32 times. Ten took 0.19 us, with POOL idle or its operation begun just behind. The other 22 took 0.52 or 1.02 to 1.14: each began 0.12 to 0.22 us behind a POOL operation of 0.62 or 1.16 to 1.31 us and ended within 0.05 us of its end. Not every operation waits so: the reciprocal of 128x4 (L3097) at 780.40 took its 0.17 us with POOL's subtraction under way since 779.83. The Trainium skill (SBUF — State Buffer, SBUF: two separate sides) calls the port pair of the two engines an exclusive lock, held for the whole instruction; the lengths of the subtractions and normalizations agree with that, the reciprocal's doesn't show it. No run isolates it.

TensorE's granted clock differed between executions of one kernel at the same time, 1.00 and 0.91 from 1200 to 1240; the work from turn (3,0)'s q to the end took 258.1 and 262.5 us. And the 256 KB of tbias, requested behind 4 MB of other loads, took 9.9 us from issue to use.
